# The last layer's block matmuls: 128 channels in fp32 and 64 channels as rounded parts stacked in the partitions

## The reference

```python
shared = _expert(xf, swg, swu, swd)            # silu(x @ wg) * (x @ wu) @ wd
...                                            # top 2 of 16 experts per token, weights comb
for e in range(E):                             # E = 16, 192 -> 384 -> 192
    routed = routed + comb[:, e:e + 1] * _expert(xf, wg[e], wu[e], wd[e])
return (shared + routed).reshape(Bq, Tq, Cq)
```

## Time and profile before

| what | us |
|---|---|
| median of 3 runs (481.32 to 487.42) | 486.88 |
| the profiled execution, its own time | 480.29 |
| its span, first to last instruction | 478.5 |
| PE busy in it | 431.8 |
| mean granted clock | 0.975 |

### The profile page before, as it was taken

The page is one execution under the profiler, slowest core; times in us unless marked ns, Lnnn a source line. Parts: engine busy times, 40 slices in busy tenths (PEclk is TensorE's granted clock), DMA queues, the critical chain, the costliest instruction groups (busy, mean ns, idle before and its releaser), DMA issues.

```text
span 478.5 us, 7595 instructions
## 1 busy us (share of the span) xinstructions
PE 431.8 (90%) x2321; PEld 308.4 (64%) x2322; DVE 223.3 (47%) x597; ACT 156.7 (33%) x394; POOL 125.1 (26%) x136
## 2 busy tenths in 40 slices
PE   0999889999999997888888779798999999999995
PEld 0755366666678886665666556446677777777775
DVE  4455342222221775789899753551443333333322
ACT  2024322222221152798787733003222221222110
POOL 3201135554551000000000000002255554444430
PEclk9999999999999999699999999869999999999999
DMA  8989011111002891000000661910011001110006
GB/s 234 264 317 276 10 34 42 43 36 40 30 17 85 227 363 76 0 1 1 3 1 0 156 142 44 269 51 8 22 35 32 22 24 36 33 31 22 0 1 197
DMA packets 18056, 38.62 MB, mean 81 GB/s; under 512 B 4420, under 2 KB 13892, under 8 KB 17586
## 3 DMA queue, kind: packets, MB, share of 16 engines
q1 hardware_dynamic: 10610, 30.45, 22.5%
q0 software_dynamic: 5280, 6.32, 4.7%
q10 hardware_dynamic: 2144, 1.57, 1.1%
HBM read 35.16 MB, written 7.67 MB: 90 GB/s over the span
## 4 chain that ended last, share of the span: by engine, by line
PE 82%; ACT 7%; DVE 4%; DMA 4%; issue 2%; DVEq 0%; SPq 0%; POOLq 0%; ACTq 0%
PE bank L1182 17%; PE bank L1197 13%; PE bank L1118 12%; PE bank L1176 8%; PE bank L1360 5%; PE bank L1189 4%; PE bank L1320 3%; PE bank L1374 3%; PE bank L1158 2%; PE bank L1104 2%; PE bank L1151 2%; ACT xn_t L673 2%; ACT scratch L673 2%; ACT g_sh L673 2%; DMA w_first<-y_rows 2%
## 5 line engine op out<-in xcount | busy, mean ns | idle before, releaser
L1182 PE MATMUL bank<-w_first,rows_t 96*128 x248 | 85.4, 487 | 0.8 <-ACT rows_t L596 0.6
L503 POOL DMA_INDIRECT rows<-xn_rows,slot_tok x56 | 57.3, 1022 | 99.8 <-DVE slot_tok L830 42.5
L511 POOL DMA_INDIRECT y_rows<-y,slot_row x54 | 55.2, 1023 | 99.0 <-DVE y L882 58.5
L1197 PE MATMUL bank<-w_second,hid_t 128*128 x370 | 70.1, 329 | 4.7 <-DVE hid_t L867 2.8
L1197 PEld LDWEIGHTS bank<-w_second,hid_t 128*128 128x128 f32 x370 | 58.7, 190 | 7.2 <-issue 7.1
L1182 PEld LDWEIGHTS bank<-w_first,rows_t 96*128 96x128 f32 x248 | 44.6, 190 | 26.1 <-issue 1.3
L872 DVE TENSOR_TENSOR act_h<-bank,act_g 128x384 f32<-128x384 f32 x31 | 17.3, 558 | 63.7 <-PE bank L1182 63.7
L1176 PE MATMUL bank<-w_first,rows_t 96*128 (+1 forms) x92 | 43.5, 594 | 1.1 <-issue 1.0
L664 ACT ACTIVATE scratch<-bank,neg_max 128x256 f32<-128x256 f32 x96 | 44.0, 478 | 0.9 <-DVE neg_max L987 0.8
L1005 DVE SCALAR_TENSOR_TENSOR scratch<-scratch,exp_inv,const 128x256 f32<-128x256 f32 x96 | 40.2, 481 | 0.8
L549 POOL COPY act_h<-o_inv 128x256 f32<-128x256 f32 x12 | 4.8, 401 | 131.1 <-DVE o_inv L1015 131.1
(11 more groups left out here) (175 smaller groups left out, 620.0 us busy)
## 6 DMA issues: line engine op xcount, KB each, us to landing
w_first<-in_gate_up SPq DMA_DIRECT2D x16, 576.0 KB, 10.0
w_second<-in_down SPq DMA_DIRECT2D x1, 4608.0 KB, 23.9
w_first<-in_fc SPq DMA_DIRECT2D x1, 3072.0 KB
w_second<-in_fc SPq DMA_DIRECT2D x1, 3072.0 KB, 28.2
xn_rows<-xn_tok SPq DMA_DIRECT2D x2, 768.0 KB, 9.5
rows<-xn_rows,slot_tok POOLq DMA_INDIRECT x56, 2.6
y_rows<-y,slot_row POOLq DMA_INDIRECT x54, 2.3
w_first<-in_x_t SPq DMA_DIRECT2D x2, 384.0 KB, 4.5
```

The source lines that it names most:

```text
L503: pool.indirect_dma_start(rows[b % 2][:], None, xn_rows[L.l], bass.IndirectOffsetOnAxis(slot_tok[:, b:b + 1].bitcast(U32), 0), bounds_chec ...
L511: pool.indirect_dma_start(y_rows[L.l], bass.IndirectOffsetOnAxis(slot_row[:, b:b + 1].bitcast(U32), 0), y[b % 2][:], None, bounds_check=TO ...
L1182: ins = pe.matmul(bank[:, 5 + g, 0:I1], rows_t[0:CH, k, :], w(CH, (k * 2 + g) * I1, I1), start=(k == 0), stop=(k == NCH - 1))
L1197: ins = pe.matmul(bank[:, 1, 0:C], hid_t[:, tile(ic)], w(P, ic * C, C), start=(ic == 0), stop=(ic == L.IC - 1))
```

## The change

Of the 192 channels, the first 128 are multiplied in fp32 with 128 rows of the array. The other 64 (`REST`) are multiplied in parts. Per block ACT copies the 64 x 768 weights of the block's expert rounded to fp32r into partitions 0 to 63 of one of two tiles (`w_parts_even`, `w_parts_odd`), and DVE writes what the rounding left into partitions 64 to 127. The token rows in DRAM get 256 columns, the last 64 channels twice, so one transpose gives them in both halves of the partitions: `rows_high` (rounded, both halves) against the stacked weights gives high*high + high*low in one matmul, and `rows_low` (64 partitions) against the high weights the third product. So `first` has two matmuls in fp32 and four in fp32r, of 384 columns each. ACT makes two copies of the transposed rows instead of one; DVE makes `rows_low`. ACT and DVE each read the block's number. The gate and up weights are loaded in two pieces per expert (32 transfers instead of 16), and the rows are stored by two transfers.

```diff
-        rows = [sb(f"rows{i}", [P, C]) for i in range(2)]
+        rows = [sb(f"rows{i}", [P, 2 * P]) for i in range(2)]
...
+        def store_rows(eng):
+            eng.dma_start(by_tile(xn_rows[1])[:, :, 0:C], xn_tok[:]).then_inc(xn_stored, 16)
+            eng.dma_start(by_tile(xn_rows[1])[:, :, C:], xn_tok[:, :, P:]).then_inc(xn_stored, 16)
...
         def act_rows(act, L, b):
             act.wait_ge(L.rows_t_ps, b + 1)
+            if L.l:
+                nc.scalar.copy(rows_t1, bank[:, 0, 0:P])
+                nc.scalar.copy(rows_high, bank[:, 0, P:2 * P]).then_inc(L.rows_t_ready, 1)
+                return
...
+        def act_part(act, L, b, u):
+            start = act.value_load(blk_weights[0:1, 0, bass.ds(b, 1)], min_val=0, max_val=(L.E - 1) * per_expert)
+            if not isinstance(b, int) or b >= 2:
+                act.wait_ge(L.up_ps, b - 1)
+            nc.scalar.copy(w_parts1[u][0:REST], rest_of(start)).then_inc(L.part_high, 1)
...
+            with act.Fori(0, (L.NB - 3) // 2) as i:
+                for u in range(2):
+                    b = i * 2 + (u + 1)
+                    act_block(act, L, b)
+                    act_rows(act, L, b + 1)
+                    act_part(act, L, b + 2, 1 - u)
...
+            def part_low(L, b, u, start):
+                dve.wait_ge(L.part_high, b + 1)
+                v.tensor_tensor(w_parts1[u][REST:], rest_of(start), w_parts1[u][0:REST].bitcast(F32), ALU.subtract
+                                ).then_inc(L.part_low, 1)
...
+            def rows_low_part(L, b):
+                dve.wait_ge(L.rows_t_ready, b + 1)
+                v.tensor_tensor(rows_low[:], bank[0:REST, 0, P:2 * P], rows_high[0:REST].bitcast(F32), ALU.subtract
+                                ).then_inc(L.rows_low_ready, 1)
...
+            def block_last(L, b, u, turn):
+                at = part_at(L, b + 1)
+                hid_copy(L, b - 1)
+                part_low(L, b + 1, u, at)
+                product(L, b)
+                rows_low_part(L, b + 1)
+                result(L, b - 1, u, turn)
...
                     for g, done in enumerate((L.first_ps, L.up_ps)):
-                        for k in range(NCH):
-                            ins = pe.matmul(bank[:, 5 + g, 0:I1], rows_t[0:CH, k, :], w(CH, (k * 2 + g) * I1, I1),
-                                            start=(k == 0), stop=(k == NCH - 1))
-                        ins.then_inc(done, 1)
+                        dst = bank[:, 5 + g, 0:I1]
+                        pe.matmul(dst, rows_t1, w(P, g * I1, I1), start=True, stop=False)
+                        if g == 0:
+                            pe.wait_ge(L.part_low, b + 1)
+                            pe.wait_ge(L.rows_low_ready, b + 1)
+                        part = w_parts1[u][:, g * I1:(g + 1) * I1]
+                        pe.matmul(dst, rows_high, part, start=False, stop=False)
+                        pe.matmul(dst, rows_low[:], part[0:REST], start=False, stop=True).then_inc(done, 1)
```

More of the change, by code:

```diff
@@ L138, in build @@
         bank = ctx.enter_context(nc.psum_tensor("bank", [P, 8, 512], F32))
-        xn_rows = [nc.dram_tensor(f"xn_rows{l}", [T, C], F32).ap() for l in range(2)]
+        ROW = (C, 2 * P)
+        xn_rows = [nc.dram_tensor(f"xn_rows{l}", [T, ROW[l]], F32).ap() for l in range(2)]
         y_rows = [nc.dram_tensor(f"y_rows{l}", [TOPK * T, C], F32).ap() for l in range(2)]
@@ L226, in build @@
         at_place = sb("at_place", [P, TOPK * NT, P], F32R)
+        with nc.sbuf_tensor("w_parts_even", [P, 2 * I1], F32R) as w_parts_even:
+            pass
         in_blk = sb("in_blk", [P, TOPK * NT, NB1 + 1], F32R)
@@ L248, in build @@
                 [xn_tok[:].rearrange("p j c -> p (j c)")[:, ic * HALF:(ic + 1) * HALF] for ic in range(I1 // P)]]
+        with nc.sbuf_tensor("w_parts_odd", [P, 2 * I1], F32R) as w_parts_odd:
+            w_parts1 = [w_parts_even[:], w_parts_odd[:]]
         xn_t_room = sb("xn_t", [P, NCH, T])
@@ L607, in act_block, with rest_of, act_blocks_last, act_blocks @@
                 nc.scalar.activation(act_g[:], bank[:, 5, 0:I1], ACT.Silu).then_inc(L.gate_act, 1)
-        def act_blocks(act, L):
-            if L.l:
-                act_rows(act, L, 0)
+        def rest_of(start):
+            return w_first[0:REST, 2 * I1:][:, 0:(E1 - 1) * per_expert + 2 * I1][:, bass.ds(start, 2 * I1)]
+        def act_part(act, L, b, u):
[3 more added lines that the diff above has]
+            nc.scalar.copy(w_parts1[u][0:REST], rest_of(start)).then_inc(L.part_high, 1)
+        def act_blocks_last(act, L):
+            act.wait_ge(L.expert_ready, len(L.sizes))
+            act.wait_ge(s_w1a, 32 * E1)
+            act.wait_ge(L.slots_ps, 1)
+            act_part(act, L, 0, 0)
+            act_rows(act, L, 0)
+            act.wait_ge(L.sh_c_ps, 2 * L.IC)
+            act_part(act, L, 1, 1)
             act_block(act, L, 0)
             act_rows(act, L, 1)
-            if L.l == 0:
-                act.wait_ge(s_qkvw, 32)
-                nc.scalar.copy(w_high, wqkv).then_inc(w_high_ready, 1)
+            act_part(act, L, 2, 0)
+            with act.Fori(0, (L.NB - 3) // 2) as i:
[4 more added lines that the diff above has]
+                    act_part(act, L, b + 2, 1 - u)
+            for b in (L.NB - 2, L.NB - 1):
+                act_block(act, L, b)
+                act_rows(act, L, b + 1)
+        def act_blocks(act, L):
+            act_block(act, L, 0)
+            act_rows(act, L, 1)
+            act.wait_ge(s_qkvw, 32)
+            nc.scalar.copy(w_high, wqkv).then_inc(w_high_ready, 1)
             with act.Fori(0, (L.NB - 1) // 2) as i:
@@ new lines, in blocks_last @@
+            def blocks_last(L):
+                dve.wait_ge(L.expert_ready, len(L.sizes))
+                dve.wait_ge(s_w1a, 32 * E1)
+                part_low(L, 0, 0, part_at(L, 0))
+                rows_low_part(L, 0)
+                part_low(L, 1, 1, part_at(L, 1))
+                product(L, 0)
+                rows_low_part(L, 1)
+                block_last(L, 1, 0, 0)
+                route(L, "diag0")
+                block_last(L, 2, 1, 0)
+                route(L, "diag1")
+                with dve.Fori(0, (L.NB - 5) // 2) as i:
+                    for u in range(2):
+                        block_last(L, i * 2 + (u + 3), u, i + 1)
+                block_last(L, L.NB - 2, 0, (L.NB - 3) // 2)
+                b = L.NB - 1
+                hid_copy(L, b - 1)
+                product(L, b)
+                result(L, b - 1, 1, (L.NB - 3) // 2)
+                hid_copy(L, b)
+                result(L, b, 0, (L.NB - 1) // 2)
@@ L1052, in _ @@
                 stage(L1, s)
-            blocks(L1)
+            blocks_last(L1)
             for j in range(NT):
@@ L1156, in rows_transpose @@
                 pe.wait_ge(L.rows_in[u], (n + 1) * 16)
+                n = P if L.l else CH
                 for k in range(NCH):
-                    ins = pe.transpose(bank[0:CH, 0, tile(k)], rows[u][:, k * CH:(k + 1) * CH], ident)
+                    ins = pe.transpose(bank[0:n, 0, tile(k)], rows[u][:, k * n:(k + 1) * n], ident)
                 ins.then_inc(L.rows_t_ps, 1)
@@ L1168, in weights, with first @@
                 return part
-            def first(L, b, w):
+            def first(L, b, w, u):
                 pe.wait_ge(L.rows_t_ready, b + 1)
@@ L1210, in blocks @@
                 else:
-                    pe.wait_ge(s_w1a, 16 * E1)
+                    pe.wait_ge(s_w1a, 32 * E1)
                     pe.wait_ge(s_w1b, 16)
-                first(L, 0, w0)
+                first(L, 0, w0, 0)
                 rows_transpose(L, 1, 1, 0)
                 hid_transpose(L, 0)
-                first(L, 1, weights(L, 1, 0))
+                first(L, 1, weights(L, 1, 0), 1)
                 rows_transpose(L, 2, 0, 1)
@@ L1219, in blocks @@
                 hid_transpose(L, 1)
-                first(L, 2, weights(L, 2, 0))
+                first(L, 2, weights(L, 2, 0), 0)
                 rows_transpose(L, 3, 1, 1)
@@ L1228, in blocks @@
                         hid_transpose(L, b - 1)
-                        first(L, b, w1)
+                        first(L, b, w1, 1 - u)
                         w2 = weights(L, b - 1, 1)
```

57 lines of the change are left out of this document (28 added, 29 removed).

## The result

The changed kernel takes 487.3 us (median of four runs, 486.4 to 489.4), the kernel before on the same chip 484.1. The ratio is 1.0145, interval [1.0095, 1.0194]: some 1.5% slower, clear of the noise but under 2%, where 2.3% faster was forecast. (Executions of one kernel fall into a faster and a slower state, and all ratios here compare the faster runs alone, so they are not quotients of the medians.) The time of 487.3 lies outside the range of 468 to 485. The profiled execution took 489.36, its span is 487.2.

What follows compares the result with a forecast made beforehand. PE was taken to bound the last layer's loop, with the gather's loop binding next. Ten pairs gaining 0.70 us and four gaining 1.14, less 0.6 at the start, save 11.0: 486.9 to 475.9 us, range 468 to 485.

Steps and rivals of the forecast that it cites:

- PE, what is saved: Last layer's `first`: two fp32 and four fp32r matmuls take 2.01 us, 0.57 less; PE alone 7.08 per two blocks.
- rival five: Fp32r passes at the pace of fp32, so PE saves nothing: 487 to 490 us; chance 0.02.
- The gather's loop: Last layer, second to scatter, gather, landing, next second: 7.32 us per two blocks, 7.52 after the change, then binding.
- these two additions: Added to the gather's loop: 0.1 us for longer gathered rows, 0.1 for POOL's steps beside DVE's low part.
- DVE and ACT: Their work per block, DVE 3.2 us and ACT 2.2, fits beside PE's 3.54, so neither is on the loop's path.
- rival four: DVE becomes the bound, 3.85 us a block: 5 us saved, 482 us; chance 0.19.
- The first blocks: Last layer's start: silu 0.8 us later, diagonal tiles lengthen two blocks' DVE sum to 4.75; together 0.6 us lost.
- Rival three: POOL and DVE block each other in the last layer's loop, 8.6 us a pair: 491 to 492 us; chance 0.07.
- the row of 1.22: A scatter beside DVE's L862 took 1.22 us instead of 1.02, read as evidence against rival three.
- The size of the gain: Whole kernel: four pairs gain 4.6 us, ten gain 7.0, less 0.6 at the start: 11.0 us saved.

Runs made afterwards that it cites:

- with 128 rows: The changed kernel with `rows_low` as a full tile of 128 partitions, its upper 64 rows zero: 469.1 us, ratio 0.9747 to the kernel before the change.

## Why the prediction was wrong, point by point

**PE, what is saved: the step that failed.** I counted the six matmuls by type and columns, 1.29 + 4 x 0.18 = 2.01, and allowed a few hundredths for fp32 and fp32r in turn. Each of those numbers holds: 2.00 with 128 rows. The term left out is the row count of the last matmul. The prediction never mentions it, so it stood at nothing without a reason. Four changes between 128 and 64 rows a block cost 4.25 - 3.54 = 0.71 us (3.54 is half a pair of 7.07, with PE alone at 128 rows), more than the 0.57 saved. That turned a gain into 0.15 lost in each steady block. The Trainium skill ("TensorEngine Tiling (Array Packing)", section "Tiling Modes") stated that a change of mode drains the engine, and the diff showed `rows_low` with 64 partitions; I weighed its rule on DVE's ports and not this one. None of the rows I read had 64 rows, but the trace before did have the sign, in attention, where matmuls of 32 rows follow such of 128:

```profile
211.75 1.09 PE L1360 MATMUL bank<-const,scratch 128*128 128x128 f32 x8
212.77 0.18 PEld L1334 LDWEIGHTS bank<-k_high,q_parts 32*128 32x128 f32 x2 [0.17 <-issue]
212.78 0.38 PE L1334 MATMUL bank<-k_high,q_parts 32*128 32x256 f32 x2
```

The load of the 32 rows starts together with its matmul, after an idle time, and that matmul starts 0.20 after the last of the eight, which follow each other at 0.12. The price for 64 rows could not be read there, but that such a term exists could.

That 487.3 lies in the 487 to 490 of rival five is luck: its mechanism, fp32r at the pace of fp32, did not come, as a pass of 384 columns took 0.17 to 0.18 and not 0.32.

**The gather's loop.** Right, but only once PE was repaired. With 128 rows the sum goes as forecast: `second` 386.91 to gather 390.80 is 3.89, landing 2.8, then 0.98 to 394.60; together 7.67 to 7.69, with 7.52 forecast and 7.1 to 7.7 measured over the gathers with rows in them, 7.07 behind them (7.08 forecast). Behind the first blocks the landing took 2.7 in the median, up to 2.9, 0.1 to 0.2 more than before, where I had taken 0.1. POOL's two steps grew by 0 and 0.02 in the median, not 0.1. I had named these two additions as what would most easily make me wrong; they did not. Whether a row of 768 bytes would land earlier was not tried.

**DVE and ACT.** Right in each duration, within 0.02: low part 0.95, rows' low part 0.28, ACT's part 0.83, its copies 0.27. Neither is on the path in the loop; rival four did not come.

**The first blocks.** Half right: silu starts 337.81 - 335.70 = 2.1 after `first` instead of 1.6, 0.5 later where I had 0.8 with block 0's saving. Two blocks near 4.7 I put down to the diagonal tiles; the long ones (5.27, 4.74) are the two after them: the first waits 0.92 for a gather, and the second comes in its wake.

**Rival three, POOL and DVE shutting each other out.** Its mechanism is real, its place is not the loop: there the scatter (385.13) starts ahead of the low part (385.66) and the gather (386.45) when it has 0.16 left. It lengthened two gathers of 32 by 0.7. I had read the row of 1.22 as 0.2 under 1.22 us of overlap, and weighed a whole block against it as if the two were rivals for one number. But only the 0.32 with the instruction that had begun first counted; they are one rule with different overlaps.

**The size of the gain.** The kernel that does what the prediction assumed has a ratio of 0.9747; 475.9 of 486.9 is 0.977. From the first `second` to the last it takes 109.5 instead of 121.5, 12.0 us less, where 11.0 had been summed. The interval, [0.9625, 0.9869], would bear a gain of anything from 1.3 to 3.8%, so the nearness of the two ratios alone proves little.

## What to carry to other kernels

Price a matmul by its row count beside its neighbours' too, not by type and columns alone: look in the trace whether the weight load begins ahead of its matmul, and if one with 64 rows stands among such of 128, fill it up with zero rows, which cost nothing here, or put the 64-row ones side by side. When a loop through another queue comes near, write down what each instruction in that queue truly waits for; here a gather stood behind a scatter it did not depend on, and changing places removed the wait (pairs of 7.05 instead of 7.69). Before trusting a price from a row, list the properties in which the new instruction differs from that row, and bound each.

## What the runs showed of the hardware

- A change between 128 and 64 rows of weights costs TensorE 0.17 to 0.19 us at a granted clock of 1.00 (2.4 GHz), as the mean of one there and one back, in fp32 (3.26 instead of 2.58 for four) as in fp32r (2.68 instead of 2.00); one between 128 and 96 nothing (1.00 for half of `first` either way).
- A matmul in fp32r of 384 columns costs 0.17 to 0.18 us, and fp32 and fp32r alternate within one sum at no cost.
- POOL's gather, held by a DVE instruction with two SBUF inputs that began first, waits to its end: 1.75 instead of 1.02 us. A scatter that begins ahead of the DVE instruction isn't slowed (1.02 to 1.03 with 0.86 of overlap).
- Some of the layer's early gathers land later than being held explains: 5.5 us after an issue of 1.73, and 4.3 after one of 1.02, where 2.7 is the rule. In both, the last of the gather's packets goes 1.3 to 1.4 after the others, beside a packet of 16 KB on the `instruction` queue; that this is the cause was not tested.
